# Even and odd queries laid out by DMA, and the gelu's last product moved from VectorE to GpSimd

## The chip, the core and the metric

The kernel runs on one core of a Trainium2 chip. Five instruction streams run side by side on the core and meet only at semaphores: PE (TensorE, matrix products and transposes), DVE (VectorE), ACT (ScalarE), POOL (GpSimd) and SP (SyncE), which here issues all DMAs. The metric is the time of one execution on the device in microseconds.

## What is computed

128 samples, each a 128 x 256 float32 matrix `x` with a context of the same shape. Cross attention with 16 heads of 16 columns comes first, then a block that is applied to three quarters of the rows of each sample:

```python
x = x + xattn(layernorm(x), ctx_1024, Wq, bq, Wkv, bkv, Wo, bo)
x = x + ffn(layernorm(x), w_router, w_block)

# xattn
q = (input @ Wq + bq);  k, v = split(encoded_features @ Wkv + bkv)
attn = softmax(q @ k.T / math.sqrt(16), axis=2)      # per head
return (attn @ v) @ Wo + bo
# ffn
scores = einsum('bld,d->bl', x, w_router)
top_idx = top_k(scores, 96)
out = x.at[top_idx].set(gelu(selected @ w_block))    # gelu: tanh form
```

## The kernel before, in words

One loop counter `s` runs from -10 to 144 on every engine, and in each step every engine does one piece of work for several samples at different stages: `scores(s)` on PE, `exps(s, j)` on ACT, `projection(s - 2)`, `block_product(s - 4)`, `final(s - 16)` on DVE and so on. Each engine's program is written out in this fixed order; nothing is scheduled at run time. A step therefore means one sample through the loop.

For the scores, four row groups of 32 partitions of PE work at once. Each group holds two heads (an even and an odd one) of one column half. To get both heads' scores from one product, `q_eo` holds the queries twice: once with the rows of odd heads zero and once with the rows of even heads zero. `q_raw` (queries plus bias) is written by DVE (`queries`, L597) for a pair of samples, and POOL multiplies it twice by `head_mask` (L764), which is 0 or 1/4, the scale of the softmax. `scores` (L292) reads `q_eo` three steps later.

The maxima of the scores (L539) are on DVE, in four parts j = 3, 2, 1, 0 per sample, and ACT's exponentials (L462) wait for each. ACT also copies attention, x1 and the transposed inputs out of PSUM.

The gelu of the block's result is spread over POOL and ACT: square (L797), factor (L804) and cubic product (L811) on POOL in step b + 5, tanh on ACT (L495) in step b + 7, and `gelu_product` (L639) on DVE in step b + 8: (tanh + 1) x z in one instruction with two inputs in SBUF. `final` (L680) on DVE in step b + 16 puts it together with the rows that are not processed (`unprocessed`, L828, on POOL).

Once for each group of 8 samples DVE finds the rows to drop (`router`): ten small steps over several values of `s`; rounds 6 to 9, the last with `keep_row` (L666), fall into one value of `s`. PE then turns `keep_row` into columns (L427).

SP loads x and context for two samples at a time and stores two samples at a time, each in the order of its own queue; each of its DMAs can wait for a semaphore, and what stands behind waits too.

Of the kernel before, what the change touches and what calls it, by code (L numbers as in the profile page):

```python
# [6 lines left out]
def cross_attention_routed_ffn(  # L7
# [20 lines left out]
    B, T, E = x.shape  # L28
# [19 lines left out]
    with ctx:  # L48
# [13 lines left out]
        q_eo = sb("q_eo", [P, 2, C, 2, 2, T])  # L62
# [19 lines left out]
        head_mask = sb("head_mask", [P, 2])  # L82
# [62 lines left out]
        parity_ready = sem("parity_ready")  # L145
        head_mask_ready = sem("head_mask_ready")
# [12 lines left out]
        q_eo_ready = sem("q_eo_ready")  # L159
# [21 lines left out]
        gelu_ready = sem("gelu_ready")  # L181
# [17 lines left out]
        def _(sp):  # L199
# [22 lines left out]

            load_x(0)
# [17 lines left out]
            for s in range(-7, LAST + 1):  # L241
                if s > -6:
                    load_c(s + 8)
                store(s - 17)
                load_x(s + 13)
# [4 lines left out]
        def _(pe):  # L250
# [22 lines left out]
            def scores(b):  # L273
# [4 lines left out]
                if h == 0:  # L278
                    pe.wait_ge(q_eo_ready, upto(b + 1))
                    pe.wait_ge(k_ready, upto(b + 1))  # L280
# [8 lines left out]
                for c in range(C):  # L289
                    for j in range(J):  # L290
                        rows = slice(32 * j, 32 * j + 32)
                        mm = nc.tensor.matmul(ps_s[:, bank(b, j), c, :, :], k_sb[rows, r2, c, h * T:(h + 1) * T],  # L292
                                              q_eo[rows, r2, c, h, :, :], start=True, stop=True)
# [151 lines left out]
        def _(act):  # L445
            def weights_high(s):
                for n, first in WEIGHTS:
                    if s == first:
                        act.wait_ge(w_in[n], 16)
                        nc.scalar.copy(w_hi[n][:, :, :], raw_w[n]).then_inc(w_hi_ready[n], 1)  # L450
# [58 lines left out]
        def _(dve):  # L509
            nc.vector.memset(v_pad[:, :, :, :, :], 0.0).then_inc(v_pad_zero, 1)  # L510

            dve.wait_ge(const_ready, 1)
            nc.vector.tensor_reduce(head_mask[:, :], ident[:, :].rearrange("p (g q d) -> p q g d", q=2, d=D), AX.XY,
                                    ALU.add).then_inc(parity_ready, 1)
            dve.wait_ge(parity_ready, 1)
            nc.vector.tensor_scalar(head_mask[:, :], head_mask[:, :], SCALE, None, ALU.mult).then_inc(head_mask_ready, 1)

            def weights_low(s):
                for n, first in WEIGHTS:
                    if s == first:  # L520
                        dve.wait_ge(w_hi_ready[n], 1)
                        nc.vector.tensor_tensor(w_lo[n][:, :, :], raw_w[n], w_hi[n][:, :, :].bitcast(f32),
                                                ALU.subtract).then_inc(w_lo_ready[n], 1)
# [65 lines left out]
            def queries(b):  # L589

                if b % 2 == 0 and has(b):
                    dve.wait_ge(q_mm, upto(b + 1))
                    if has(b - 4):
                        dve.wait_ge(q_eo_ready, upto(b - 3))
                    if b == 0:
                        dve.wait_ge(b_in, 64)
                    nc.vector.tensor_tensor(q_raw[:, (b // 2) % 2, :, :, :].rearrange("p c b t -> p c (b t)"),  # L597
# [36 lines left out]

            def gelu_product(b):

                if has(b):
                    dve.wait_ge(tanh_ready, upto(b))
# [228 lines left out]
```

## Time and profile before

| what | us |
|---|---|
| median of 3 runs | 970.96 |
| lowest and highest run | 969.74, 970.99 |
| the profiled execution | 971.5 |
| its span, first to last instruction | 969.6 |
| mean granted TensorE clock, share of full speed | 0.986 |

The profile gives each instruction's start and length and the event that ended the idle time before it. "Busy" is the time in which an engine has an instruction in progress; ACT's and PE's instructions overlap, so their lengths add up to more than their busy time. Timeline rows read: start, length, engine, line, operation, what is written from what. Rows from SPq are DMA issues on SP's queue. Busy time by itself does not say what bounds the loop, since the engines wait for each other within a step.

### The profile page before, as it was taken

To read this page: it belongs to the slowest core of one execution; us is meant where nothing else is said; L and a number is where in the kernel's file an instruction comes from. 1 tells how busy PE (TensorE), PEld (TensorE's weight loads), DVE (VectorE), ACT (ScalarE), POOL (GpSimd) and SP (SyncE) were. 2 spreads that over 40 slices of the span, in tenths; PEclk is the share of its full clock that TensorE was granted. 3 is DMA by queue.
4 is the path that set the end of the run, shared out by engine and by line. 5 is a ranking of instruction groups with operands and counts; after the bars stand their busy time and mean duration, and the time that the engine had idled before them with its cause. 6 is when DMAs were issued, how large, how long until landed. Compare 5 with 4: busy or idle time off the path is not lost. (4 is left out here: it accounts for less than half of the span.)

```text
span 969.6 us, 32620 instructions
## 1 busy us (share of the span) xinstructions
PE 901.8 (93%) x10276; PEld 756.4 (78%) x10276; DVE 916.4 (95%) x2696; ACT 898.4 (93%) x4612; POOL 827.0 (85%) x1386
## 2 busy tenths in 40 slices
PE   3799999999999999999999999999999999999971
PEld 3688888878788888888888887888878788788750
DVE  4689999999999999999999999999999999999975
ACT  2699999999999999999999999999999999999970
POOL 5567889999898898989989899998989999998757
PEclk9899999999999999999999999999999999999995
DMA  7010111122122122112212212211211221210002
GB/s 213 5 45 24 45 46 52 50 67 68 34 67 67 36 67 67 49 54 67 67 35 67 67 34 67 67 47 55 67 48 55 67 67 35 67 46 23 13 24 87
DMA packets 54857, 53.99 MB, mean 56 GB/s; under 512 B 4000, under 2 KB 54688, under 8 KB 54688
## 3 DMA queue, kind: packets, MB, share of 16 engines
q1 hardware_dynamic: 54688, 51.92, 17.0%
q8 instruction: 84, 1.38, 0.6%
q14 instruction: 85, 0.70, 0.2%
HBM read 35.13 MB, written 16.78 MB: 54 GB/s over the span
## 5 line engine op out<-in xcount | busy, mean ns | idle before, releaser
L462 ACT ACTIVATE e_sb<-ps_s,neg_max 128x128 f32<-128x128 f32 x2048 | 717.5, 413 | 14.9 <-DVE neg_max L539 14.6
L462 ACT ACTIVATION_READ_ACCUMULATOR e_sb<-ps_s,neg_max 128x1 f32 x2048 | 516.3, 253 | 0.0
L539 DVE TENSOR_REDUCE neg_max<-ps_s 128x4 f32<-128x512 f32 x512 | 328.0, 660 | 21.0 <-PE ps_s L292 19.3
L292 PE MATMUL ps_s<-q_eo,k_sb 32*128 32x256 f32 x2048 | 147.6, 401 | 8.8 <-ACT e_sb L462 5.3
L764 POOL TENSOR_TENSOR q_eo<-q_raw,head_mask 128x512 f32<-128x512 f32 x128 | 141.5, 1124 | 2.6 <-PE ps_t L313 1.6
L265 PE MATMUL ps_a<-w_o_sb,o_sb 128*128 128x256 f32 x512 | 137.6, 391 | 5.4 <-DVE v_sb L621 2.7
L776 POOL TENSOR_TENSOR v_pad<-v_sb,recip 128x256 f32<-128x256 f32 x128 | 79.4, 620 | 71.7 <-DVE recip L577 71.3
L341 PE MATMUL ps_a<-e_sb,v_pad 128*32 128x128 f32 x4096 | 138.4, 276 | 0.7 <-DVE x_sb L547 0.6
L265 PE MATMUL ps_t<-w_z_sb,xt_sb 128*128 128x258 f32 x512 | 134.0, 384 | 3.6 <-DVE z_sb L632 3.6
L292 PEld LDWEIGHTS ps_s<-q_eo,k_sb 32*128 32x128 f32 x2048 | 96.3, 185 | 38.0 <-issue 36.5
L341 PEld LDWEIGHTS ps_a<-e_sb,v_pad 128*32 128x32 f32 x4096 | 104.1, 109 | 22.4 <-issue 21.3
L753 POOL TENSOR_TENSOR x_sb<-x_sb,bo_sb 128x256 f32<-128x256 f32 x128 | 106.6, 833 | 9.5
L265 PEld LDWEIGHTS ps_t<-w_z_sb,xt_sb 128*128 128x128 f32 x512 | 96.0, 191 | 20.0 <-issue 4.9
L265 PEld LDWEIGHTS ps_a<-w_o_sb,o_sb 128*128 128x128 f32 x512 | 86.9, 189 | 21.1 <-issue 11.8
L811 POOL TENSOR_TENSOR g_sb<-g_sb,z_sb 128x256 f32<-128x256 f32 x128 | 99.4, 776 | 0.8
L473 ACT CAST t_hi<-ps_t 128x512 fp32r<-128x512 f32 x128 | 76.0, 594 | 25.1 <-PE ps_t L313 23.9
L584 DVE TENSOR_TENSOR t_lo<-ps_t,t_hi 128x512 fp32r<-128x512 f32 x128 | 86.6, 676 | 1.8 <-ACT t_hi L473 1.8
L258 PE MATMUL ps_a<-w_v_hi,t_hi 128*128 128x256 f32 x256 | 83.6, 327 | 2.7 <-ACT o_sb L481 2.5
L639 DVE SCALAR_TENSOR_TENSOR z_sb<-g_sb,z_sb 128x256 f32<-128x256 f32 x128 | 84.0, 657 | 0.0
L744 POOL TENSOR_SCALAR xhat<-x_sb,neg_m,rstd 128x256 f32<-128x256 f32 x128 | 81.9, 640 | 0.1
L797 POOL TENSOR_TENSOR g_sb<-z_sb 128x256 f32<-128x256 f32 x128 | 79.0, 617 | 3.1 <-DVE z_sb L632 3.0
L680 DVE SCALAR_TENSOR_TENSOR z_sb<-z_sb,half_keep,x_sb 128x256 f32<-128x256 f32 x128 | 72.1, 564 | 7.0 <-POOL x_sb L828 7.0
(80 smaller groups left out, 2252.2 us busy)
## 6 DMA issues: line engine op xcount, KB each, us to landing
x_sb<-in_x SPq DMA_DIRECT2D x64, 256.0 KB, 3.0
c_sb<-in_ctx SPq DMA_DIRECT2D x64, 256.0 KB, 3.1
out<-z_sb SPq DMA_DIRECT2D x64, 256.0 KB, 2.2
z_sb<-in_L_xattn_Wkv SPq DMA_DIRECT2D x2, 256.0 KB, 5.7
z_sb<-in_L_xattn_Wq SPq DMA_DIRECT2D x1, 256.0 KB, 3.0
w_o_sb<-in_L_xattn_Wo SPq DMA_DIRECT2D x1, 256.0 KB, 7.5
w_z_sb<-in_L_ffn_w_block SPq DMA_DIRECT2D x1, 256.0 KB, 5.6
bv_sb<-in_L_xattn_bkv SPq DMA_DIRECT2D x1, 128.0 KB, 3.5
```

What stands on the lines that cost most here:

```text
L258: last = nc.tensor.matmul(dst, lhs(a, c), rhs(b, c), start=(c == 0 and n == 0), stop=(c == C - 1 and n == len(terms) - 1))
L265: last = nc.tensor.matmul(dst, lhs(c), rhs(c), start=(c == 0), stop=(c == C - 1))
L292: mm = nc.tensor.matmul(ps_s[:, bank(b, j), c, :, :], k_sb[rows, r2, c, h * T:(h + 1) * T], q_eo[rows, r2, c, h, :, :], start=True, stop=True)
L341: mm = nc.tensor.matmul(ps_attn[32 * j:32 * j + 32, c * T:(c + 1) * T], v_pad[:, b % 2, c * J + j, par:par + 2, :].rearrange("p a d -> p ( ...
L462: last = nc.scalar.activation(e_sb[:, b % 4, j, c, par, :], ps_s[:, bank(b, j), c, par, :], ACT.Exp, bias=neg_max[:, b % 4, h:h + 1], accu ...
L539: nc.vector.tensor_reduce(neg_max[:, b % 4, :].rearrange("p (c j q) -> p j c q", c=C, j=J)[:, j, :, :], ps_s[:, bank(b, j), :, :, :], AX.X ...
L584: nc.vector.tensor_tensor(t_lo[part].rearrange("p k c t -> p (k c) t"), ps_t[:, :].rearrange("p (n t) -> p n t", t=T), t_hi[part].rearrang ...
L639: nc.vector.scalar_tensor_tensor(z_sb[:, b % R, 0:E], g_sb[:, b % 4, :], 1.0, z_sb[:, b % R, 0:E], ALU.add, ALU.mult).then_inc(gelu_ready, 1)
L744: nc.gpsimd.tensor_scalar(xhat[:, b % 4, :], x_sb[:, r, :], neg_m1[:, r:r + 1], rstd1[:, r:r + 1], ALU.add, ALU.mult).then_inc(xhat_ready, 1)
L753: nc.gpsimd.tensor_tensor(x_sb[:, b % R, :], x_sb[:, b % R, :], bo_sb[:, :], ALU.add).then_inc(xb_ready, 1)
L764: last = nc.gpsimd.tensor_tensor(q_eo[:, n, :, :, par, :], q_raw[:, n, :, :, :], head_mask[:, par:par + 1].rearrange("p (a b c) -> p a b c ...
L811: nc.gpsimd.tensor_tensor(g_sb[:, b % 4, :], g_sb[:, b % 4, :], z_sb[:, b % R, 0:E], ALU.mult).then_inc(cubic_ready, 1)
```

## The change

The layout of `q_eo` becomes parity first, so that one head parity's rows are contiguous in a partition (2 KB). It is zeroed once by DVE. For each pair of samples, SP then copies the 16 partitions of each parity of each row group from `q_raw` into it: 8 DMAs of 16 partitions x 512 elements. The scale 1/4 moves into the weights (`w_hi`, `w_lo`) and the bias of the queries; `head_mask` goes. `queries` waits for the DMAs of the pair before it in the same buffer, and `scores` for all eight. `gelu_product` leaves DVE; POOL gets `gelu_sum` (tanh + 1, in place) and `gelu_product`, both in step b + 7.

```diff
-        q_eo = sb("q_eo", [P, 2, C, 2, 2, T])
+        q_eo = sb("q_eo", [P, 2, 2, C, 2, T])
...
+            def queries_even_odd(b):
+
+                if b % 2 == 0 and has(b):
+                    n = (b // 2) % 2
+                    if b == 0:
+                        sp.wait_ge(q_eo_zero, 1)
+                    sp.wait_ge(q_raw_ready, upto(b + 1))
+                    if has(b - 4):
+                        sp.wait_ge(s_mm[J - 1], upto(b - 3))
+                    for par in range(2):
+                        for j in range(J):
+                            rows = slice(32 * j + D * par, 32 * j + D * par + D)
+                            sp.dma_start(q_eo[rows, n, par, :, :, :], q_raw[rows, n, :, :, :]).then_inc(q_eo_in[n], 16)
...
             for s in range(-7, LAST + 1):
+                queries_even_odd(s + 3)
                 if s > -6:
                     load_c(s + 8)
                 store(s - 17)
...
-                    pe.wait_ge(q_eo_ready, upto(b + 1))
+                    pe.wait_ge(q_eo_in[r2], (b // 4 + 1) * 128)
...
-                                              q_eo[rows, r2, c, h, :, :], start=True, stop=True)
+                                              q_eo[rows, r2, :, c, h, :], start=True, stop=True)
...
-                        nc.scalar.copy(w_hi[n][:, :, :], raw_w[n]).then_inc(w_hi_ready[n], 1)
+                        nc.scalar.activation(w_hi[n][:, :, :], raw_w[n], ACT.Copy,
+                                             scale=SCALE if n == "q" else 1.0).then_inc(w_hi_ready[n], 1)
...
-            dve.wait_ge(const_ready, 1)
-            nc.vector.tensor_reduce(head_mask[:, :], ident[:, :].rearrange("p (g q d) -> p q g d", q=2, d=D), AX.XY,
-                                    ALU.add).then_inc(parity_ready, 1)
-            dve.wait_ge(parity_ready, 1)
-            nc.vector.tensor_scalar(head_mask[:, :], head_mask[:, :], SCALE, None, ALU.mult).then_inc(head_mask_ready, 1)
+            nc.vector.memset(q_eo[:, :, :, :, :, :], 0.0).then_inc(q_eo_zero, 1)
...
                     if has(b - 4):
-                        dve.wait_ge(q_eo_ready, upto(b - 3))
+                        dve.wait_ge(q_eo_in[(b // 2) % 2], b // 4 * 128)
                     if b == 0:
                         dve.wait_ge(b_in, 64)
+                        nc.vector.tensor_scalar(bq_sb[:, :], bq_sb[:, :], SCALE, None, ALU.mult).then_inc(bq_scaled, 1)
+                        dve.wait_ge(bq_scaled, 1)
...
-            def gelu_product(b):
-
-                if has(b):
-                    dve.wait_ge(tanh_ready, upto(b))
-                    nc.vector.scalar_tensor_tensor(z_sb[:, b % R, 0:E], g_sb[:, b % 4, :], 1.0, z_sb[:, b % R, 0:E],
-                                                   ALU.add, ALU.mult).then_inc(gelu_ready, 1)
...
                 stats1(s + 10)
-                gelu_product(s - 8)
                 aggregate2(s - 3)
...
-                    for par in range(2):
-                        last = nc.gpsimd.tensor_tensor(q_eo[:, n, :, :, par, :], q_raw[:, n, :, :, :],
-                                                       head_mask[:, par:par + 1].rearrange("p (a b c) -> p a b c", a=1, b=1).to_broadcast([P, C, 2, T]),
-                                                       ALU.mult)
-                    last.then_inc(q_eo_ready, 2)
...
+            def gelu_sum(b):
+
+                if has(b):
+                    pool.wait_ge(tanh_ready, upto(b))
+                    nc.gpsimd.tensor_scalar(g_sb[:, b % 4, :], g_sb[:, b % 4, :], 1.0, 1.0,
+                                            ALU.add, ALU.mult).then_inc(gelu_sum_ready, 1)
+
+            def gelu_product(b):
+
+                if has(b):
+                    pool.wait_ge(gelu_sum_ready, upto(b))
+                    nc.gpsimd.tensor_tensor(z_sb[:, b % R, 0:E], g_sb[:, b % 4, :], z_sb[:, b % R, 0:E],
+                                            ALU.mult).then_inc(gelu_ready, 1)
...
                 gelu_factor(s - 5)
+                gelu_sum(s - 7)
                 input_and_bias(s + 4)
                 gelu_cubic(s - 5)
-                queries_even_odd(s + 3)
+                gelu_product(s - 7)
```

POOL in the middle of the program, before, from one `v_pad` to the next, in a step of odd number (names are written tile, then what it is computed from; `x2` is two in a row):

```order
L776 TENSOR_TENSOR v_pad<-v_sb,recip 128x8x2x16
L828 TENSOR_SCALAR x_sb<-x_sb,alpha,beta 128x256
L804 TENSOR_SCALAR g_sb<-g_sb 128x256
L753 TENSOR_TENSOR x_sb<-x_sb,bo_sb 128x256
L811 TENSOR_TENSOR g_sb<-g_sb,z_sb 128x256
L764 TENSOR_TENSOR q_eo<-q_raw,head_mask 128x4x128 x2
L744 TENSOR_SCALAR xhat<-x_sb,neg_m,rstd 128x256
```

The same place of POOL after the change (each step has these rows):

```order
L768 TENSOR_TENSOR v_pad<-v_sb,recip 128x8x2x16
L834 TENSOR_SCALAR x_sb<-x_sb,alpha,beta 128x256
L796 TENSOR_SCALAR g_sb<-g_sb 128x256
L810 TENSOR_SCALAR g_sb<-g_sb 128x256
L758 TENSOR_TENSOR x_sb<-x_sb,bo_sb 128x256
L803 TENSOR_TENSOR g_sb<-g_sb,z_sb 128x256
L817 TENSOR_TENSOR z_sb<-g_sb,z_sb 128x256
L749 TENSOR_SCALAR xhat<-x_sb,neg_m,rstd 128x256
```

The two `q_eo` rows of every second step are gone; L810 and L817, the sum and the product of the gelu, stand in every step.

SP in the middle, before, for two pairs of samples:

```order
L213 DMA c_sb<-in_ctx 128x2x256
L220 DMA out<-z_sb 128x2x256
L205 DMA x_sb<-in_x 128x2x256
L213 DMA c_sb<-in_ctx 128x2x256
L220 DMA out<-z_sb 128x2x256
L205 DMA x_sb<-in_x 128x2x256
```

SP at the same place after:

```order
L212 DMA c_sb<-in_ctx 128x2x256
L234 DMA q_eo<-q_raw 16x512 x8
L219 DMA out<-z_sb 128x2x256
L204 DMA x_sb<-in_x 128x2x256
L212 DMA c_sb<-in_ctx 128x2x256
L234 DMA q_eo<-q_raw 16x512 x8
L219 DMA out<-z_sb 128x2x256
L204 DMA x_sb<-in_x 128x2x256
```

Eight small DMAs stand ahead of each pair's store and load of x.

POOL near the end, after the change, from the last square on:

```order
L789 TENSOR_TENSOR g_sb<-z_sb 128x256
L834 TENSOR_SCALAR x_sb<-x_sb,alpha,beta 128x256
L796 TENSOR_SCALAR g_sb<-g_sb 128x256
L810 TENSOR_SCALAR g_sb<-g_sb 128x256
L803 TENSOR_TENSOR g_sb<-g_sb,z_sb 128x256
L817 TENSOR_TENSOR z_sb<-g_sb,z_sb 128x256
L834 TENSOR_SCALAR x_sb<-x_sb,alpha,beta 128x256
L810 TENSOR_SCALAR g_sb<-g_sb 128x256
L817 TENSOR_TENSOR z_sb<-g_sb,z_sb 128x256
L834 TENSOR_SCALAR x_sb<-x_sb,alpha,beta 128x256
L810 TENSOR_SCALAR g_sb<-g_sb 128x256
L817 TENSOR_TENSOR z_sb<-g_sb,z_sb 128x256
```

Before, three of the `x_sb` rows (L828) followed each other here without a gelu instruction between them.

## Rows read from the trace of the kernel before

**Rows 1.** part 1 of the page, busy us and share of each engine
```profile
PE 901.8 (93%) x10276; PEld 756.4 (78%) x10276; DVE 916.4 (95%) x2696; ACT 898.4 (93%) x4612; POOL 827.0 (85%) x1386
```

**Rows 2.** windows: length, busy us of PE, PEld, DVE, ACT, POOL; clock, DMA
```profile
63.37:132.37 69.00, 68.39 (x805) 58.45 (x801) 62.58 (x181) 68.74 (x361) 55.51 (x95) 1.00 0.13 40
139.44:888.74 749.30, 731.90 (x8428) 615.06 (x8428) 744.71 (x2196) 734.16 (x3783) 677.54 (x1127) 1.00 0.18 56
```

**Rows 3.** timeline of PE: start us, us, the scores of six samples
```profile
63.37 1.15 PE L292 MATMUL ps_s<-q_eo,k_sb 32*128 32x256 f32 x16
...
132.37 1.15 PE L292 MATMUL ps_s<-q_eo,k_sb 32*128 32x256 f32 x16
...
139.44 1.15 PE L292 MATMUL ps_s<-q_eo,k_sb 32*128 32x256 f32 x16 [0.15 <-issue]
...
538.66 1.15 PE L292 MATMUL ps_s<-q_eo,k_sb 32*128 32x256 f32 x16
...
546.95 1.15 PE L292 MATMUL ps_s<-q_eo,k_sb 32*128 32x256 f32 x16
...
888.74 1.15 PE L292 MATMUL ps_s<-q_eo,k_sb 32*128 32x256 f32 x16
```

**Rows 4.** timeline of DVE in the long step
```profile
539.25 0.74 DVE L666 TENSOR_SCALAR keep_row<-cand 8x128 f32<-8x128 f32 x1
...
540.25 1.11 DVE L639 SCALAR_TENSOR_TENSOR z_sb<-g_sb,z_sb 128x256 f32<-128x256 f32 x1
...
541.50 1.24 DVE L539 TENSOR_REDUCE neg_max<-ps_s 128x4 f32<-128x512 f32 x2
```

**Rows 5.** ACT in the long step; then waits: us in total, times, longest
```profile
542.18 0.37 ACT L462 ACTIVATE e_sb<-ps_s,neg_max 128x128 f32<-128x128 f32 x1 [1.16 <-DVE neg_max L539]
...
ACT e_sb L462 <- DVE neg_max L539: 14.6, 15, 1.2
```

**Rows 6.** timeline of DVE, an early step; idle before it in brackets
```profile
92.17 1.29 DVE L539 TENSOR_REDUCE neg_max<-ps_s 128x4 f32<-128x512 f32 x2 [0.68 <-PE ps_s L292]
```

**Rows 7.** groups of 300:700 us: busy us, mean ns of one
```profile
L764 POOL TENSOR_TENSOR q_eo<-q_raw,head_mask 128x512 f32<-128x512 f32 x56 | 62.1, 1127 | 0.0
L811 POOL TENSOR_TENSOR g_sb<-g_sb,z_sb 128x256 f32<-128x256 f32 x56 | 44.0, 787 | 0.0
L639 DVE SCALAR_TENSOR_TENSOR z_sb<-g_sb,z_sb 128x256 f32<-128x256 f32 x56 | 38.2, 683 | 0.0
L804 POOL TENSOR_SCALAR g_sb<-g_sb 128x256 f32<-128x256 f32 x56 | 22.7, 405 | 4.7
```

**Rows 8.** waits of POOL, 139.44:888.74: us in total, times, longest
```profile
POOL v_pad L776 <- DVE recip L577: 42.3, 65, 1.5
```

**Rows 9.** SP's queue in a step; then DMA issues, us to landing
```profile
525.26 0.50 SPq L213 DMA_DIRECT2D c_sb<-in_ctx  x1
...
x_sb<-in_x SPq DMA_DIRECT2D x64, 256.0 KB, 3.0
out<-z_sb SPq DMA_DIRECT2D x64, 256.0 KB, 2.2
```

**Rows 10.** timelines of DVE, PE and DVE at the start
```profile
21.64 0.69 DVE L597 TENSOR_TENSOR q_raw<-ps_q,bq_sb 128x512 f32<-128x512 f32 x1 [1.31 <-PE ps_q L258]
...
27.93 1.15 PE L292 MATMUL ps_s<-q_eo,k_sb 32*128 32x256 f32 x16
...
28.71 0.42 DVE L565 BATCH_NORM_STATS2 st<-x_sb 128x6 f32<-128x256 f32 x1
```

**Rows 11.** timelines of POOL and DVE in the drain
```profile
946.16 0.19 POOL L787 TENSOR_TENSOR ve<-mv,eps_sb 128x2 f32<-128x2 f32 x1 [1.58 <-DVE mv L559]
...
954.77 3.15 POOL L828 TENSOR_SCALAR x_sb<-x_sb,alpha,beta 128x256 f32<-128x256 f32 x3
...
958.92 0.21 DVE L666 TENSOR_SCALAR keep_row<-cand 8x128 f32<-8x128 f32 x1
...
960.31 6.04 POOL L828 TENSOR_SCALAR x_sb<-x_sb,alpha,beta 128x256 f32<-128x256 f32 x8
```

More of the change, by code:

```diff
@@ L81, in cross_attention_routed_ffn @@
         minus_mean = sb("minus_mean", [P, P])
-        head_mask = sb("head_mask", [P, 2])
         eps_sb = sb("eps_sb", [P, 2])
@@ L144, in cross_attention_routed_ffn @@
         v_pad_zero = sem("v_pad_zero")
-        parity_ready = sem("parity_ready")
-        head_mask_ready = sem("head_mask_ready")
+        bq_scaled = sem("bq_scaled")
         w_hi_ready = {n: sem(f"w_{n}_hi_ready") for n in "qkv"}
@@ L158, in cross_attention_routed_ffn @@
         q_raw_ready = sem("q_raw_ready")
-        q_eo_ready = sem("q_eo_ready")
+        q_eo_zero = sem("q_eo_zero")
+        q_eo_in = [sem(f"q_eo_in{i}") for i in range(2)]
         k_mm = sem("k_mm")
@@ L180, in cross_attention_routed_ffn @@
         tanh_ready = sem("tanh_ready")
-        gelu_ready = sem("gelu_ready")
+        gelu_ready, gelu_sum_ready = sem("gelu_ready"), sem("gelu_sum_ready")
         score_mm = sem("score_mm")
@@ L521, in weights_low @@
                         dve.wait_ge(w_hi_ready[n], 1)
-                        nc.vector.tensor_tensor(w_lo[n][:, :, :], raw_w[n], w_hi[n][:, :, :].bitcast(f32),
-                                                ALU.subtract).then_inc(w_lo_ready[n], 1)
+                        nc.vector.scalar_tensor_tensor(w_lo[n][:, :, :], raw_w[n], SCALE if n == "q" else 1.0,
+                                                       w_hi[n][:, :, :].bitcast(f32), ALU.mult,
+                                                       ALU.subtract).then_inc(w_lo_ready[n], 1)
                 if s == 0:
@@ L723, in _ @@
                                     pattern=[[-1, P]], channel_multiplier=1).then_inc(const_ready, 1)
-            pool.wait_ge(head_mask_ready, 1)
             pool.wait_ge(v_pad_zero, 1)
@@ L754, in input_and_bias @@
                                             ALU.add).then_inc(xb_ready, 1)
-            def queries_even_odd(b):
-                if b % 2 == 0 and has(b):
-                    pool.wait_ge(q_raw_ready, upto(b + 1))
-                    if has(b - 4):
-                        pool.wait_ge(s_mm[J - 1], upto(b - 3))
-                    n = (b // 2) % 2
-                    for par in range(2):
-                        last = nc.gpsimd.tensor_tensor(q_eo[:, n, :, :, par, :], q_raw[:, n, :, :, :],
-                                                       head_mask[:, par:par + 1].rearrange("p (a b c) -> p a b c", a=1, b=1).to_broadcast([P, C, 2, T]),
-                                                       ALU.mult)
-                    last.then_inc(q_eo_ready, 2)
             def values_over_sums(b):
```

## The prediction

> **What bounds the kernel now.** I read part 1 of the page first. PE, ACT and DVE are each busy for 93 to 95% of the span and POOL for 85% [rows 1], so no share names the bound; the stage has to be read. The middle of the program is 105 steps, from the scores that start at 139.44 to those at 888.74 [rows 3]: 749.3 us, 7.136 a step. In it DVE is busy for 744.7 us, 99.4%, ACT for 734.2, POOL for 677.5 [rows 2]. An earlier stretch shows the same loop before the router and the final step begin: ten steps from 63.37 to 132.37 take 69.00 us, 6.90 a step. There ACT is busy for 68.74 of 69.00 us, and DVE sits idle before its first maximum of a step (0.68 us in the row) [rows 2, 3, 6]. So ACT, with its 16 exponentials and four copies a sample, sets a floor of 6.90, and in the middle DVE adds to it.
>
> Where it adds: once per group of 8 samples the four router instructions (last two rounds and keep_row) fall into one step, and that step takes 8.29 us instead of about 6.9 (538.66 to 546.95) [rows 3]. DVE comes to its maxima only at 541.50, behind keep_row (0.74) and the gelu product (1.11) [rows 4], and ACT waits 1.16 us for neg_max; all such waits sum to 14.6 us, 15 times, and 12 of them have this length [rows 5]. The other 93 steps take (749.3 - 12 x 8.29) / 93 = 6.987.
>
> **Taken from DVE.** One gelu product a step, 56 in the stretch of 400 us at 683 ns [rows 7]. DVE's need falls from 744.7 / 105 = 7.09 us a step to 6.41, under the floor of 6.90. In the router step the product that goes is 1.11 us long [rows 4], almost all of the 1.16 that ACT waits, and DVE no longer enters that step late. So the step time should fall to between 6.90 (ACT's floor) and 6.987 plus nothing (ordinary steps keep their present length, the 12 long ones become ordinary). The ordinary steps' excess of 0.09 has one cause that I can see, a DVE with no idle time, so part of it should go as well; I take the middle, 6.945. That gives 105 x 6.945 = 729.2, a gain of 20.1. The ends are 24.8 (6.90) and, with 6.987 and a remainder of 0.3 in each of 12 groups, 749.3 - 733.6 - 3.6 = 12.
>
> **POOL: out and in.** Out go two q_eo products for every two samples, 1127 ns each, so 1.13 a step. In come gelu_sum, which has the form of the gelu factor (405 ns), and gelu_product, which has the form of the cubic product (787 ns) [rows 7], with some 0.08 for one more hand-over: 1.27. POOL's present need is its busy time and its gaps without the waits for recip: (749.3 - 42.3) / 105 = 6.73 [rows 2, 8]. After: 6.73 - 1.13 + 1.27 = 6.87. This is 0.03 under ACT's floor, so the bound moves from one engine to nearly two. The load also becomes even, where q_eo stood in every second step only. The wait for v_pad has a cushion, since attention is PE's last work of a step.
>
> POOL's cubic product and DVE's gelu product show each other's presence: the product's mean is 683 ns and reaches 1.11 us beside q_eo [rows 4, 7]. The Trainium skill (SBUF — State Buffer, Who interferes with whom) says that a DVE instruction with two SBUF inputs and a GpSimd instruction that reads SBUF exclude each other for their whole length. By that rule, the trace agrees, removing the product from DVE also shortens POOL's own rows; the sum stays, the chance of the POOL rival falls.
>
> **Queries by DMA.** Eight DMAs of 32 KB for each pair replace the POOL work; the mask and the scale are prepared once in weights and bias, at no steady cost. SP issues them ahead of the store and of load_x. An issue occupies SP for about 0.5 us [rows 9], so 8 take 4 us of the 13.9 us that a pair lasts, and SP has nothing else but three issues. q_raw of sample s+3 is written in step s and read in step s+3: at least two whole steps, 13.8 us, lie between, and 4 + 3.0 us for a landing [rows 9] fit. No row shows an SBUF to SBUF DMA; the nearest are the 256 KB ones with 2.2 and 3.0 us. The bound below is nothing, above is 13.8 - 7 = 6.8 us of room. Behind these issues wait the store and the loads; these have three steps until their use, so 4 us are hidden. If that cover went, each pair would pay what is over. PE reads q_eo in two pieces of 128 columns, now 2 KB apart, instead of 256 in a row. No row has such a read; I take zero, and PE, under its full load, could hide little above that.
>
> **Start.** q_raw(0) starts at 21.64 and is done at 22.3; two small steps for the scaled bias add 0.2. Eight issues end at 26.5, and the landing (2.2 to 3.0) makes q_eo(0) ready at 28.2 to 29.5, where scores(0) start at 27.93 today. The load of x(10) queues behind them and lands at 26.6 + 3.0 = 29.6, where DVE reads it at 28.71 [rows 9, 10]. The first maxima stand behind it. From here to the first exponentials nothing is idle in their favour, so this costs 0.3 to 2 us; I take 1.0. DVE's memset of q_eo is over about when x(0) lands.
>
> **Drain.** After the last scores POOL's own chain sets the end: it waits for DVE at 946.16 (1.58 us), and then works without a wait to the last of three u products at 957.92; keep_row follows at 958.92 and then eight more u products [rows 11]. Here each added pair of gelu instructions (0.405 + 0.08 + about 0.70) lies on the path, since z, the candidates and the last router rounds wait for DVE's final, and that for u. Five such pairs lie between 946.16 and the last of the three u (those of steps 130 to 134): 5 x 1.19 = 5.95. Against it stands that the three u take 3.15 us today, because DVE's chain beside them is slow, where three of eight later ones would take 3 x 0.755 = 2.27, and that four gelu products leave DVE. I take 4.5, with 2 and 5 as ends.
>
> **Sum.** -20.1 + 1.0 + 4.5 = -14.6. The profiled execution has a span of 969.6 and 971.5 us with what lies around it; the median of the runs is 970.96, 0.5 lower. So the span becomes 955.0, the profiled time 956.9, and the median 956.4.
>
> **Rivals.** (1) POOL becomes the bound. For it: 6.87 stands next to 6.90, and its rows stretch when others run beside them (the cubic product's mean of 787 ns). At 7.0 a step: 105 x 7.0 = 735.0, gain 14.3, median 970.96 - 14.3 + 5.5 = 962.2. Against: the wait for recip today sums to 42.3 us and the work added is 0.14 a step, 15 us in 105 steps. The Trainium skill (GPSIMD Engine Reference, 4.1 Engine selection) speaks against the move: elementwise work belongs on VectorE, since GpSimd takes about twice as long for two inputs. An estimate by that page, 2 x 683 ns for the product, makes POOL's need 7.45, and the time then about 1009 us; the row of the same form says 787.
> (2) Slower: POOL's need passes 7.10. There the middle takes 105 x 7.10 = 745.5, a gain of 3.8 that start and drain (5.5) more than eat; at 7.25 the middle takes 761.3 and the time is 970.96 + 12 + 5.5 = 988. The point is reached where POOL's five two-input instructions a step (square, v_pad, bias, cubic, product) stretch by 0.05 each beyond their present means. Nothing in the rows suggests it, but the slack is thin.
> (3) SP's queue becomes the bound: 11 issues in 13.9 us allow 1.26 us each. At 1.4 us, 64 pairs x 1.5 us = +96 us. The row says 0.5.
> (4) Only the long steps shrink and the ordinary ones keep 6.987 with a remainder: gain 12 to 15.6, median 961 to 964.
> That the change doesn't do what it says is out: the order of POOL and SP shows it.
>
> **Chances.** Forecast 0.55; (1) 0.17; (4) 0.14; (2) 0.07; (3) 0.02; a gain eaten until within 0.2% 0.05. The predicted time is 956.4. The range must hold the forecast's own ends (24.8 - 2.3 = 22.5, so 948.5; 12 - 7 = 5, so 966) and rivals (1) and (4): 949 to 966. About 2 us, 0.2%, is what a measurement can tell from no change. Faster 0.87, same 0.05, slower 0.08.
>
> **What would show it.** In the middle, the step of 8.29 should be gone and ACT's wait for neg_max with it; the step near 6.94; ACT busy above 99%; DVE idle again before its first maximum; POOL busy at about 95%, with q_eo rows gone and its wait for recip short but there. SP's eight issues of 0.5 us should end well ahead of the scores. The first scores should start near 28.9, and the span from the last neg_max to the end should be 4 to 5 us longer, with POOL in the chain. Wrong would be: waits of PE for v_pad or for a DMA, POOL without waits at over 6.95 a step, or the product at over 0.9 us.

## The result and the profile after

| | before | after |
|---|---|---|
| median of 4 runs, us | 970.35 | 957.89 |
| lowest and highest run | 969.64, 970.99 | 957.61, 958.20 |
| ratio after / before, 95% interval | | 0.9875 [0.9861, 0.9890] |
| span of the profiled execution | 969.6 | 956.0 |
| granted TensorE clock | 0.986 | 0.985 |

The change is faster by 1.25%, 12.5 us in the medians; the two profiled executions lie 13.6 us apart in their spans, because the profiled one of the kernel before was about 1 us above its median. The profile shows where. First part 1 of the page of the kernel after (busy us and share of each engine, answering [rows 1]), then the window over the same 105 steps of the middle (length; busy us of PE, PEld, DVE, ACT, POOL; clock, DMA share, GB/s; answering the second line of [rows 2]):

```profile
PE 892.5 (93%) x10276; PEld 757.0 (79%) x10276; DVE 849.6 (89%) x2568; ACT 894.6 (94%) x4612; POOL 814.4 (85%) x1514
```
```profile
140.22:871.17 730.95, 724.02 (x8427) 616.81 (x8427) 687.53 (x2091) 729.83 (x3783) 666.37 (x1231) 1.00 0.27 77
```

The 105 steps take 730.95 us, 6.961 each, where they took 749.30. DVE fell from 99.4% to 94.1% of the stretch. The scores of a router group, from the timeline of PE (start, length, engine, line, operation):

```profile
592.81 1.15 PE L306 MATMUL ps_s<-q_eo,k_sb 32*128 32x256 f32 x16
599.74 1.15 PE L306 MATMUL ps_s<-q_eo,k_sb 32*128 32x256 f32 x16
606.52 1.15 PE L306 MATMUL ps_s<-q_eo,k_sb 32*128 32x256 f32 x16
613.61 1.15 PE L306 MATMUL ps_s<-q_eo,k_sb 32*128 32x256 f32 x16 [0.16 <-issue]
```

The pattern of a group is 7.12, 6.93, 6.78, 7.09, 6.88, 6.98, 6.78, 7.09; the step of 8.29 [rows 3] is gone. ACT waits for neg_max 1.0 us in the whole program, where one such wait was 1.16 [rows 5]. DVE now waits for the scores before its first maximum, also in the middle, and POOL still waits a little for recip (waits of the 105 steps, 140.22:871.17: us in total, times, longest):

```profile
DVE neg_max L551 <- PE ps_s L306: 38.1, 69, 0.9
POOL v_pad L768 <- DVE recip L589: 37.1, 91, 1.4
```

The groups of the stretch 300:700 us (busy us, mean ns of one, idle before), as in [rows 7]: the new product is L817, the new sum L810, the cubic product L803, the bias addition L758, the step's one DVE instruction that still reads two tiles of SBUF is `final`, L687.

```profile
L758 POOL TENSOR_TENSOR x_sb<-x_sb,bo_sb 128x256 f32<-128x256 f32 x58 | 57.7, 994 | 0.0
L803 POOL TENSOR_TENSOR g_sb<-g_sb,z_sb 128x256 f32<-128x256 f32 x58 | 40.7, 702 | 0.0
L817 POOL TENSOR_TENSOR z_sb<-g_sb,z_sb 128x256 f32<-128x256 f32 x58 | 39.4, 680 | 0.0
L687 DVE SCALAR_TENSOR_TENSOR z_sb<-z_sb,half_keep,x_sb 128x256 f32<-128x256 f32 x57 | 30.1, 528 | 0.0
L810 POOL TENSOR_SCALAR g_sb<-g_sb 128x256 f32<-128x256 f32 x57 | 23.2, 407 | 4.6
```

The queries' DMAs on SP's queue in the middle, and the page's row on their issues (count, KB each, median us from issue to landing), answering [rows 9]:

```profile
541.83 5.55 SPq L234 DMA_DIRECT2D q_eo<-q_raw  x8
547.42 0.58 SPq L219 DMA_DIRECT2D out<-z_sb  x1
```
```profile
q_eo<-q_raw SPq DMA_DIRECT2D x512, 32.0 KB, 2.0
```

Eight issues take 5.55 us here, 0.69 each. After the store and the two loads SP then issues nothing for 6.5 us until the next eight, and no wait of PE for them stands in the middle.

The start (answering [rows 10]), from the timelines of SP and of PE:

```profile
21.99 5.01 SPq L234 DMA_DIRECT2D q_eo<-q_raw  x8
```
```profile
28.42 1.15 PE L306 MATMUL ps_s<-q_eo,k_sb 32*128 32x256 f32 x16 [1.29 <-DMA q_eo<-q_raw]
```

The drain (answering [rows 11]), from the timeline of POOL:

```profile
929.32 0.20 POOL L779 TENSOR_TENSOR ve<-mv,eps_sb 128x2 f32<-128x2 f32 x1 [0.39 <-DVE mv L571]
...
940.53 0.56 POOL L834 TENSOR_SCALAR x_sb<-x_sb,alpha,beta 128x256 f32<-128x256 f32 x1
941.05 0.40 POOL L810 TENSOR_SCALAR g_sb<-g_sb 128x256 f32<-128x256 f32 x1
941.54 0.77 POOL L817 TENSOR_TENSOR z_sb<-g_sb,z_sb 128x256 f32<-128x256 f32 x1
...
943.99 0.55 POOL L834 TENSOR_SCALAR x_sb<-x_sb,alpha,beta 128x256 f32<-128x256 f32 x1
```

The last scores start at 911.41 (before 929.13), so 44.6 us lie behind them, where 40.5 did. In the drain POOL waits 0.39 us instead of 1.58 and then works through to the last of the three u rows (943.99 + 0.55), with a sum and a product between each two of them.

The account of the span: middle -18.35; start +0.78 (scores number 16 start at 140.22 instead of 139.44); the six steps between the middle and the last scores -0.15 (40.24 instead of 40.39); drain +4.1. Together -13.6, which is 956.0 - 969.6. Of the 18.35, 12 x (8.29 - 7.12) = 14.0 come from the twelve long steps, which are now steps of 7.12, and 4.3 from the other 93, which went from 6.987 to (730.95 - 12 x 7.12) / 93 = 6.941.

### The profile page after: what moved, and what is told of

It is laid out like the page before. It is cut to its first block, busy times and chain, and to the rows that moved or that the text cites. A ratio compares the mean times of both kernels' runs of the same rounds, so it can differ in the third digit from the quotient of the medians.

```text
span 956.0 us, 33133 instructions
## 1 busy us (share of the span) xinstructions
PE 892.5 (93%) x10276; PEld 757.0 (79%) x10276; DVE 849.6 (89%) x2568; ACT 894.6 (94%) x4612; POOL 814.4 (85%) x1514
## 4 chain that ended last, share of the span: by engine, by line
PE 88%; ACT 5%; issue 2%; POOL 2%; DVE 1%; SPq 1%; DMA 1%; POOLq 0%; ACTq 0%; DVEq 0%
PE ps_q L272 18%; PE ps_s L306 14%; PE ps_a L355 13%; PE ps_a L279 12%; PE ps_t L279 11%; PE ps_a L272 9%; PE ps_t L327 8%; ACT e_sb L477 4%; PE ps_q L342 3%; DMA x_sb<-in_x 1%; POOL x_sb L834 1%; SPq L234 0%; POOL z_sb L817 0%; DVE neg_max L551 0%; PE ps_t L441 0%
## 5 line engine op out<-in xcount | busy, mean ns | idle before, releaser
L477 ACT ACTIVATE e_sb<-ps_s,neg_max 128x128 f32<-128x128 f32 x2048 | 724.9, 459 | 1.2 <-DVE neg_max L551 1.0
L477 ACT ACTIVATION_READ_ACCUMULATOR e_sb<-ps_s,neg_max 128x1 f32 x2048 | 588.3, 299 | 0.0
L551 DVE TENSOR_REDUCE neg_max<-ps_s 128x4 f32<-128x512 f32 x512 | 332.0, 669 | 64.4 <-PE ps_s L306 62.2
L758 POOL TENSOR_TENSOR x_sb<-x_sb,bo_sb 128x256 f32<-128x256 f32 x128 | 121.3, 947 | 0.2
L488 ACT CAST t_hi<-ps_t 128x512 fp32r<-128x512 f32 x128 | 80.9, 632 | 25.0 <-PE ps_t L327 23.8
L803 POOL TENSOR_TENSOR g_sb<-g_sb,z_sb 128x256 f32<-128x256 f32 x128 | 90.7, 709 | 0.0
L817 POOL TENSOR_TENSOR z_sb<-g_sb,z_sb 128x256 f32<-128x256 f32 x128 | 87.6, 684 | 0.2
L510 ACT ACTIVATE g_sb<-g_sb 128x256 f32<-128x256 f32 x128 | 74.1, 579 | 8.2 <-POOL g_sb L803 8.2
L687 DVE SCALAR_TENSOR_TENSOR z_sb<-z_sb,half_keep,x_sb 128x256 f32<-128x256 f32 x128 | 67.7, 529 | 11.5 <-POOL x_sb L834 11.5
L834 POOL TENSOR_SCALAR x_sb<-x_sb,alpha,beta 128x256 f32<-128x256 f32 x128 | 73.0, 571 | 1.7
```

Of the source, the lines that this page charges most:

```text
L477: last = nc.scalar.activation(e_sb[:, b % 4, j, c, par, :], ps_s[:, bank(b, j), c, par, :], ACT.Exp, bias=neg_max[:, b % 4, h:h + 1], accu ...
L488: nc.scalar.copy(t_hi[:, n, :, :, h * T:(h + 1) * T].rearrange("p k c t -> p (k c) t"), ps_t[:, :].rearrange("p (n t) -> p n t", t=T)).the ...
L551: nc.vector.tensor_reduce(neg_max[:, b % 4, :].rearrange("p (c j q) -> p j c q", c=C, j=J)[:, j, :, :], ps_s[:, bank(b, j), :, :, :], AX.X ...
L758: nc.gpsimd.tensor_tensor(x_sb[:, b % R, :], x_sb[:, b % R, :], bo_sb[:, :], ALU.add).then_inc(xb_ready, 1)
L803: nc.gpsimd.tensor_tensor(g_sb[:, b % 4, :], g_sb[:, b % 4, :], z_sb[:, b % R, 0:E], ALU.mult).then_inc(cubic_ready, 1)
L817: nc.gpsimd.tensor_tensor(z_sb[:, b % R, 0:E], g_sb[:, b % 4, :], z_sb[:, b % R, 0:E], ALU.mult).then_inc(gelu_ready, 1)
```

## The experiments

Two things were open after this. The change has two halves, and DVE's need falls by both (the product itself; the q_eo products that stretch DVE's rows). And the prediction says that ACT is the floor and POOL next to it. Each kernel's scores were read in the same way as above: "middle" is the 105 steps from scores number 16 on, "drain" what lies from the last scores to the end of the span. Ratios are to the kernel before, with the 95% interval. One-run times have no interval. Four chips were used: a first for the DMA half alone, the move alone and the kernel before without the product; a second for the full change again, the full change with more POOL, the one with the last 8 products on DVE and the DMA half with the load of x(10) first; a third for the DMA half alone again, the two kernels with POOL's two extra instructions and the one without tanh; a fourth for both repairs. The full change reads 957.89 and 955.90 in its two timings, so 2 us between rows of different chips say nothing by themselves.

| kernel | median us (runs) | ratio | middle | drain |
|---|---|---|---|---|
| before | 970.3 to 971.3 | 1 | 749.3 | 40.5 |
| full change | 957.89 (4) | 0.9875 [0.9861, 0.9890] | 730.95 | 44.6 |
| full change, again | 955.90 (4) | 0.9849 [0.9835, 0.9862] | 729.5 | 43.6 |
| DMA half alone | 955.23 (4) | 0.9841 [0.9825, 0.9858] | 729.7 | 41.6 |
| DMA half alone, again | 954.98 (5) | 0.9848 [0.9835, 0.9861] | 730.8 | 40.4 |
| move alone | 1000.99 (1) | | 777.4 | 43.8 |
| before without the product | 952.51 (4) | 0.9810 [0.9796, 0.9825] | 731.0 | 40.5 |
| DMA half, POOL keeps reading | 971.76 (1) | | 749.35 | 40.4 |
| DMA half, POOL only writes | 959.47 (1) | | 737.2 | 40.4 |
| full change, more POOL | 959.05 (1) | | 729.4 | 47.0 |
| full change without tanh | 950.68 (1) | | 725.95 | 43.6 |
| full change, last 8 products on DVE | 952.56 (4) | 0.9816 [0.9803, 0.9830] | 729.2 | 40.5 |
| DMA half, load of x(10) first | 951.83 (5) | 0.9809 [0.9796, 0.9822] | 729.4 | 40.4 |
| both repairs on the full change | 953.81 (5) | 0.9832 [0.9819, 0.9846] | 731.0 | 40.5 |

### The DMA half alone

```diff
             for s in range(FIRST, LAST):
                 stats1(s + 10)
+                gelu_product(s - 8)        # one instruction on DVE, as before
...
-                gelu_sum(s - 7)
...
-                gelu_product(s - 7)
```

> The queries are laid out by DMA as in the changed kernel; the gelu product stays on DVE in one instruction, in step b + 8. Theory (DVE was the bound, and part of its length was waiting beside POOL's q_eo products): the product shortens from 683 ns to about 0.45 us, keep_row from 0.74 to about 0.2, the step of 8.29 us loses most of its excess, the ordinary steps stay near 6.99. Middle 105 x 7.0 = 735, gain 14, start +0.8, no longer drain: median about 957 to 960, and DVE busy still 97% or more. Rival A (DVE's rows have their lengths in any case, the DMA part only makes room on POOL): the product stays at 0.65 us or more, the long step stays at 8.2, median 970 to 972. Rival B (POOL's q_eo was the bound): ACT is busy in over 98.5% of the middle and DVE gets idle time, median below 955.

Measured: 955.23 us, and 954.98 when repeated; below the 957 to 960 of the theory, since the ordinary steps shrank too. The window of the 105 steps (columns as above) of the repeated run:

```profile
140.68:871.46 730.78, 725.73 (x8427) 617.23 (x8428) 721.56 (x2195) 730.03 (x3783) 554.50 (x1021) 1.00 0.27 77
```

DVE still does the product and is busy 98.7% of the stretch, yet the steps are as short as with the full change. The product on DVE lasts 414 ns in place of the 683 of [rows 7]. So the DMA half carries the whole gain of the middle. For DVE's length of a step, taking POOL's q_eo products away did what taking the product away was meant to do.

> The same kernel as e1_dma_alone, timed again with more rounds since its four runs lay between 952.9 and 955.5. Theory (its middle equals that of the full change and its drain is 4 us shorter; the moved load at the start is worth little, as scores(2) start at 43.0 against 43.3 in the traces): 951.5 to 953 us, 3 to 4 us below the full change's 955.9. Rival (the first median was its level, and the moved load is worth 3 us): 954.5 to 955.5.

The 954.98 is the rival's value, not the theory's. Against its kernel before, the DMA half alone is at 0.9841 and 0.9848, the full change at 0.9875 and 0.9849: no gain of the product's move can be seen on top of the DMA half, in the time or in the middle.

### The product's move alone, and the product left out

```diff
-                gelu_product(s - 8)        # DVE
...
+                gelu_sum(s - 7)            # POOL, beside the q_eo products
+                gelu_product(s - 7)
```

> The queries stay on POOL; only the gelu's sum and product move to POOL. Theory (POOL had 6.73 us of work in a step of 7.14): POOL's need becomes 6.73 + 0.41 + 0.68 + 0.08 = 7.9 us a step, POOL has no wait for recip left, PE and ACT wait for it: middle 105 x 7.9 = 830, median 1045 to 1065. Rival (POOL has more room than its rows say, since rows overlap the waits): median 957 to 975.

Measured: 1000.99 us in one run, against 971.32 for the kernel before on that chip, between the two ranges that were written down; steps of 7.40 in the mean. The waits of the middle (us in total, times, longest) show the rival that the full change escaped, POOL as the bound:

```profile
DVE z_sb L673 <- POOL x_sb L834: 68.7, 52, 1.6
...
PE ps_a L341 <- POOL v_pad L768: 39.2, 51, 1.1
```

POOL has no wait in it; its rows, with what waiting they hold, fill the 7.40 us. The move by itself is thus 3% slower, and it is borne only where the DMA half goes with it; even there it brings nothing in the middle (729.5 to 731.0 against 729.7 to 730.8) and lengthens the drain. The step of 7.9 that I had written was too long; some of POOL's own rows were shorter than in [rows 7]: the cubic product 682 ns, not 787, q_eo 1039, not 1127.

```diff
-                gelu_product(s - 8)        # DVE; no other engine does it
```

> The kernel before with the gelu's last product left out altogether (that part of the computation is missing), q_eo on POOL as before. Theory (DVE was the bound, POOL's load of 6.73 is below the floor of 6.90): the step of 8.29 goes, steps of 6.93 to 6.96, middle 728 to 731, gain 18 to 21 with nothing lost at the start and 0 to 2 us won in the drain: median 949 to 953. Rival (the gain of the changed kernel came from POOL's relief of q_eo, not from DVE): little change, 964 to 971.

This kernel leaves out the gelu's last product, so its result isn't the reference's.

Measured: 952.51 us, as the theory had it, the middle 731.0. keep_row still lasts 0.74 there, so the product's 1.11 us was enough to take the long step away. With q_eo still on POOL, taking the product from DVE also gives the step of 6.96. Either half of the relief is enough for the middle. They are not two gains that add up.

### Is it POOL's reading that stretches DVE?

Both kernels are the DMA half alone, with two more POOL instructions for each pair of samples, where the q_eo products stood; nobody reads what they write. One pair reads `q_raw` as the q_eo products did, the other only writes. In both kernels DVE's `queries` waits for the earlier pair of them (not in the cuts below); the profile shows no wait of DVE for it in the middle of the first. The layout by DMA stays in both, so neither it nor the hand-over through POOL can be what differs.

```diff
+                    for par in range(2):
+                        last = nc.gpsimd.tensor_tensor(junk[..., par, ...], q_raw[:, n, :, :, :], eps_sb[:, par:par + 1]..., ALU.mult)
```
```diff
+                    for par in range(2):
+                        last = nc.gpsimd.memset(junk[:, n, 1024 * par:1024 * par + 1024], 0.0)
```

> As e1_dma_alone, but POOL still multiplies q_raw twice a pair at its old place, into a tile that nobody reads. Theory (two products of POOL that read SBUF hold back the gelu product and keep_row on DVE): the product is back at 0.65 to 0.7 us, the step of 8.2 to 8.3 us is back once in 8, middle 745 to 750, median 968 to 973. Rival (it was the hand-over through POOL, or the layout, that cost): as e1_dma_alone, 951 to 956.

> As e13_pool_keeps_reads, but POOL's two idle instructions only write (memset of 1024 columns each, about 1 us each) and read nothing from SBUF. Theory (DVE's instruction with two SBUF inputs and POOL's reads exclude each other, writes alone don't): the product stays near 0.42 us, no long step, steps 6.96, median 951 to 956. Rival (any work of POOL beside DVE stretches it, or POOL's time counts as such): as e13_pool_keeps_reads, 965 to 973.

Measured, one run each: 971.76 us with the reads, in the theory's range; 959.47 with writes only, between the theory's range and the rival's. With the reads the gain is gone to the last tenth. The middle takes 749.35 us (before 749.30), the group has its step of 8.28 again. The timeline of PE, then of DVE and of POOL in that step:

```profile
539.34 1.15 PE L307 MATMUL ps_s<-q_eo,k_sb 32*128 32x256 f32 x16
547.62 1.15 PE L307 MATMUL ps_s<-q_eo,k_sb 32*128 32x256 f32 x16
```
```profile
539.92 0.74 DVE L682 TENSOR_SCALAR keep_row<-cand 8x128 f32<-8x128 f32 x1
...
540.92 1.11 DVE L655 SCALAR_TENSOR_TENSOR z_sb<-g_sb,z_sb 128x256 f32<-128x256 f32 x1
```
```profile
539.54 2.22 POOL L779 TENSOR_TENSOR junk<-q_raw,eps_sb 128x512 f32<-128x512 f32 x2
```

These are the 0.74 and the 1.11 of [rows 4]. In the same place of the kernel without POOL's two products the timeline of DVE reads:

```profile
530.98 0.21 DVE L680 TENSOR_SCALAR keep_row<-cand 8x128 f32<-8x128 f32 x1
...
531.46 0.40 DVE L653 SCALAR_TENSOR_TENSOR z_sb<-g_sb,z_sb 128x256 f32<-128x256 f32 x1
```

The ends line up. POOL's first product ends at 539.54 + 1.11 = 540.65, and keep_row, issued at 539.92, ends at 540.66. POOL's second ends at 541.76, and DVE's product ends 0.27 behind it. So each of the two DVE instructions comes to its end only behind the POOL instruction that it met. In the long step that was 0.53 + 0.71 = 1.24 us, for a wait of ACT of 1.16. (keep_row beside other rows of POOL takes 0.27 in most groups of the kernel without the two products, and 0.43 in the full change.)

With writes only the middle takes 737.2. The product on DVE stays short (449 ns in the mean; of the 57 between 300 and 700 us, 25 lie beside a memset alone and last 0.40), but keep_row is held up, in some groups by both memsets:

```profile
532.53 1.84 POOL L779 MEMSET junk<- 128x1024 f32 x2
```
```profile
532.92 1.52 DVE L682 TENSOR_SCALAR keep_row<-cand 8x128 f32<-8x128 f32 x1
```

Here keep_row ends at 534.44, 0.07 behind the memsets, and a product issued behind it (533.39, 1.05 us) ends with it: a row can also hold the wait of the row ahead of it. Six of the 14 steps of the middle in this place of the group take 7.77 us, the others 7.12, where keep_row mostly takes 0.62; another step of each group takes 7.20 in place of 7.02, and why is not read here. So the theory holds for the product, and fails for keep_row. That the middle is 12 us shorter than with the reads fits a product that is no longer stretched; the memsets are also shorter than the products (0.95 against 1.13 us), and the runs don't separate the two.

The Trainium skill (SBUF — State Buffer, Who interferes with whom) has both cases: two SBUF inputs on DVE collide with a GpSimd instruction that reads SBUF and not with one that only writes, while a DVE `tensor_scalar` in a two-port mode collides with any, for the whole instruction. The rows agree for the product, 683 ns beside reads against 449. For keep_row, a `tensor_scalar`, they fit as well, 0.74 and 1.52 against 0.21 us; which mode it ran in, no row shows.

### How near is POOL to being the bound?

```diff
                     pool.wait_ge(gelu_sum_ready, ...)
+                    nc.gpsimd.tensor_scalar(g_sb[:, b % 4, :], g_sb[:, b % 4, :], 1.0, 0.0, ALU.mult, ALU.add)...
```

> The full change with one more POOL instruction of 0.41 us a step (the sum is copied onto itself). Theory (POOL's need is about 6.6 us, of the step's 6.96, the wait for recip of 0.34 us a step is its whole room): need 7.05 to 7.15, POOL's wait for recip gone, steps of about 7.05 to 7.15: median 968 to 980, drain 2 us longer among it. Rival (POOL had more room than the wait shows): steps stay at 6.96, median 959 to 961.

Measured: 959.05 us, the rival's value. The middle stays at 729.4 us, 6.95 a step (729.5 for the full change on the same chip), although 0.40 us of work were added to each step and POOL's wait for recip is 0 in the stretch 300:700. The bias addition, which stood at 994 ns in the full change (1001 on this chip), is:

```profile
L758 POOL TENSOR_TENSOR x_sb<-x_sb,bo_sb 128x256 f32<-128x256 f32 x58 | 45.5, 784 | 0.0
```

So POOL's rows hold waiting inside them, which work can take the place of. Per step, the wait for recip gave 0.33 us and this row 0.22, while the sum's row (L810) grew from 0.40 to 0.53. What the bias addition waited for can be read in the full change, from the timelines of DVE and POOL:

```profile
612.33 0.48 DVE L687 SCALAR_TENSOR_TENSOR z_sb<-z_sb,half_keep,x_sb 128x256 f32<-128x256 f32 x1
```
```profile
612.44 0.95 POOL L758 TENSOR_TENSOR x_sb<-x_sb,bo_sb 128x256 f32<-128x256 f32 x1
```

It ends 0.58 us behind `final`, DVE's other instruction with two inputs in SBUF. Between 300 and 700 us 43 of its rows start while `final` is in progress, and each ends 0.58 to 0.60 behind it. Here POOL is the one that is held up. The price of the added instruction stands in the drain alone, 47.0 us against 43.6 (on the same chip 959.05 against 955.90).

### Is ACT the floor?

```diff
-                gelu_tanh(s - 7)
...
-                    pool.wait_ge(tanh_ready, upto(b))
+                    pool.wait_ge(cubic_ready, upto(b))
```

> The full change without the tanh on ACT (left out; the sum takes the cubic product instead). Question: what bounds the steps of 6.96 that all variants reach. Theory PE (the chain of the full change's trace is 88% PE): steps stay at 6.94 to 6.96, ACT shows idle time of 0.3 us a step, median 953 to 957. Rival ACT (16 exponentials and four copies fill it): 0.32 us a step less on ACT, steps fall to PE's 6.80 or below, median 935 to 942.

This kernel leaves out the tanh, so what it computes isn't the gelu.

Measured: 950.68 us in one run, below the theory's 953 to 957 and far above the rival's; the window of the 105 steps:

```profile
138.99:864.94 725.95, 722.52 (x8428) 615.69 (x8428) 684.99 (x2091) 706.87 (x3678) 665.07 (x1231) 1.00 0.27 77
```

The step falls by 0.048 only, to 6.914, though a tanh of 0.59 us (mean of its rows in the full change) left ACT. PE is now busy for 99.5% and ACT for 97.4%, and ACT now waits for PE, where the middle of the full change shows no wait of ACT:

```profile
ACT t_hi L488 <- PE ps_t L327: 17.8, 79, 0.4
```

The pattern of a group becomes 7.12, 6.93, 6.78, 6.93, 6.88, 6.93, 6.78, 6.93: the steps of 7.09 and 6.98 shrink to 6.93 and the others keep their length. So ACT adds 0.05 to 0.16 in three steps of eight and doesn't bound the other five. PE is what is left for those: it waits for another engine once, 0.3 us, while DVE and ACT wait for it. No run took work from PE, so this is read from the trace and not tested. ACT's busy share of 99.8% in the full change did not say that: its accumulator reads have a mean of 305 ns there, 255 here, and 248 in the kernel before.

### The drain and the start

```diff
+        LATE = B - 8
...
-                if has(b):                 # gelu_sum, gelu_product on POOL
+                if 0 <= b < LATE:
...
                 router(s - 15, 9)
+                gelu_product(s - 8)        # DVE, for b >= LATE, one instruction
```

> The changed kernel, but the gelu's sum and product of the last 8 samples (120 to 127) are one instruction on DVE again, at the end of its step b + 8. Theory (the added POOL instructions lie on the chain of the drain): the time from the last scores to the end falls from 44.6 us to 40 to 41.5, the median from 957.9 to about 954 to 955. Rival (the drain's 4 us come from something else, the router's chain or the stores): median stays at 957 to 958.5.

> The full change again, beside the others on one chip, as their comparison. Theory and rival alike: 957.5 to 958.5 us, ratio to the kernel before 0.986 to 0.989; e1_dma_alone and e11_dma_alone_start are below it by 2.5 to 4 us if the drain is what the moved product costs.

Measured on the same chip: 952.56 against 955.90 us, drain 40.5 against 43.6, as the theory had the drain. The 955.90 itself is 2 us under what was expected of a repeat; its middle is 1.4 us shorter than the first time and its drain 1.0. POOL's timeline has its three u rows in one piece again:

```profile
935.03 3.15 POOL L845 TENSOR_SCALAR x_sb<-x_sb,alpha,beta 128x256 f32<-128x256 f32 x3
```

So the drain's price is that of the gelu work on POOL, and it can be had back.

```diff
             for s in range(-7, LAST + 1):
+                if s == -3:
+                    load_x(s + 13)
                 queries_even_odd(s + 3)
```

> The queries by DMA and the gelu product on DVE (as e1_dma_alone), and the load of x(10) stands ahead of the first eight q_eo DMAs on SP. Theory (DVE's first maxima waited for that load, 2.29 us in the changed kernel's trace, where the scores were only 0.5 us late): scores(1) 0.8 to 1.3 us earlier, median 0.5 to 1.3 us below e1_dma_alone's 955.2: 954 to 954.7. Rival (the late q_eo(0) sets the start): no difference, 955 to 955.5.

> The full change with both repairs together: the last eight samples' gelu product as one instruction on DVE, and the load of x(10) and x(11) ahead of the first eight q_eo DMAs. Theory A: the moved load is worth the 3 us that lay between the two kernels with the DMA alone (951.83 with it, 954.98 and 955.23 without); then the median is 952.56 - 3 = 949.5, the ratio near 0.978, and the scores with number 16 start 1 to 3 us before the 139.89 of the kernel without it. Rival B: the start differs from run to run by about a microsecond whatever this load does (scores number 16 start at 139.46 and 140.68 in two profiles of one kernel, 139.71 with the load moved); then the median stays within a microsecond of 952.5 (ratio 0.981 to 0.982), and scores number 16 start between 139.4 and 140.7. Both: 105 steps of the middle in 729 to 731 us, and 40.4 from the last scores to the end.

The DMA half with this load moved gave 951.83 us, under both expectations and 3 less than without it; but that one ran on another chip, and scores number 16 start at 139.71, and at 139.46 and 140.68 in the two profiles of the kernel without it. Put on top of the repaired drain it gave 953.81, not the 949.5 that a worth of 3 us would mean, and 0.3 above what rival B allowed; the middle is 731.0 there and scores number 16 start at 139.46. So theory A has fallen and the load's place is worth nothing that can be seen. The start has a spread of its own: scores(0) start at 27.93 before and at 26.70 with the product left out, and the two programs are the same up to there. What makes the 3 us between 951.83 and 954.98 isn't settled; the middle differs by 1.4 us of it between the profiles, and one kernel's middle read 729.7 and 730.8 in two runs. All four kernels with the DMA half on the second chip read 729.2 to 729.5, so the chip may be part of it.

## Why the prediction was right, and where it was not

The time, 957.89 for 956.4, came out inside the range, by a sum whose terms hold and whose reasons hold in part. From profile to profile the forecast was -14.6 and the measured sum -13.6: the middle gave 1.75 us less than forecast, and start, drain and the steps between together 0.8 less loss, so small misses also cancel.

**The long step.** It went, with ACT's wait, as forecast. The forecast said that the product's 1.11 us leaves the step, and the kernel without the product shows that this suffices. The runs show more: of 1.11 and 0.74 only 0.40 and 0.21 were DVE's own work, and the rest was POOL's q_eo product, which left too. I had read the two rows as showing "each other's presence" and then drew from it only a smaller chance for the POOL rival. It was what made the step long, and by it the half of the change that I costed at nothing on DVE gives the whole gain alone.

**The ordinary steps.** Forecast 6.945, measured 6.961: the gain of the middle 18.35, not 20.1, inside 12 to 24.8. The mis-sized term is the floor. ACT's 6.90 comes from before the router. In the middle the steps take 6.914 without the tanh, with two longer ones in each group (7.12, in which PE turns keep_row into columns, and 6.88, instead of 6.93 and 6.78 beside them), and ACT adds 0.05. The twelve long steps could thus fall to 7.12 and not to the "ordinary" 6.987 or less that the forecast gave them. The "excess of 0.09" that I gave to a DVE without idle time is mostly this. After the change DVE idles and the excess over 6.90 is 0.06.

**ACT above 99%.** 99.8%, as said, but no proof of a bound: without the tanh only 0.048 us a step were had.

**POOL.** Forecast need 6.87, product 787 ns, sum 405, busy 95%. Measured: (730.95 - 37.1) / 105 = 6.61, 680, 407 and 91%. Busy time less waits overstated POOL's need, in the kernel before as in the move alone (7.40 measured where 6.73 + 1.27 = 8.00), because its rows contain waiting for DVE; the bias addition shows it, 994 ns with room and 784 without, with its end tied to `final`'s. The 6.61 is for the same reason still above the true need. Rival (1) at 7.0 and rival (2) past 7.10 were further off than the 6.87 made them look: 0.40 us more did not reach the first, though it used up the wait for recip. POOL's own rows did get shorter without the product on DVE, as forecast: the cubic product has a mean of 702 ns in the full change, 787 before and 864 where the DMA half stands alone. That GpSimd takes about twice as long for two inputs (the Trainium skill, GPSIMD Engine Reference, 4.1 Engine selection) comes out here as 1.6, 680 against 414 ns. The estimate of 1009 us doubled the 683 ns, a product stretched by POOL. With its sum the work takes 1.09 us on POOL, against the 0.41 of DVE's one instruction.

**DMAs.** Landing 2.0 us against 2.2 to 3.0; an issue 0.62 to 0.69 us, not 0.5, so 5 to 5.6 us for eight, still hidden. Rival (3) did not come. PE's split read of q_eo cost nothing: the mean row of the scores in the stretch 300:700 is 399 ns before and after.

**Start.** +0.78 against +1.0, first scores at 28.42 against 28.9. The term is right in size and cannot be called shown; that it came out is luck: the same code started its first scores 1.2 us apart in two kernels, and scores number 16 start at 137.1 to 139.4 in the three kernels with q_eo on POOL and at 139.0 to 140.7 in those with the DMAs.

**Drain.** +4.1 against +4.5, in the place named: five pairs of sum and product on POOL between its last wait for DVE and the last of the three u rows. From that wait to the end of the three it took 11.76 us before and 15.22 after; POOL comes to this place 0.9 later behind the last scores (17.9 us against 17.0), and what follows the three is 0.2 shorter. The kernel with these products on DVE got all of it back.

**Rival (4)** is closer to the truth than its place as a rival suggests: the ordinary steps shrank from 6.987 to 6.941 only, 4.3 us in all, and 14.0 of the 18.35 are the long steps. Its remainder did not come, so the time stayed below its 961.

## What to carry to other kernels

When a row on DVE is longer than its kind (keep_row 0.74 against 0.21, the product 683 against 414 ns), look for the GpSimd row whose end it shares. Take that one away, and DVE has its time back without losing any of its work; here that alone gave all that the middle had to give, and the product could have stayed where it was. A busy share doesn't say what an engine needs: before an engine is called a floor or full, take a piece of its work away or add one, as ACT (0.59 less, 0.05 gained) and POOL (0.40 more, nothing lost in the loop) showed here. And price a move twice, for the loop and for the drain, where the engine that receives it may end last.

## What the runs showed of the hardware

A copy from SBUF to SBUF of 16 partitions x 2 KB lands 2.0 us after its issue, and eight in a row hold SP for 5.0 to 5.6 us. They brought the core's DMA share from 18 to 27% in the middle, at no visible cost to the loads (x lands in 2.9 us, before 3.0); stores land in 2.4 us, before 2.2. A GpSimd memset, which reads nothing, held up an 8 x 128 `tensor_scalar` of DVE from 0.21 to 0.62 us, and to 1.52 across two memsets, while the two-input product beside a memset stayed at 0.40. A GpSimd addition of 128 x 256 that starts within a two-input instruction of DVE ends 0.58 to 0.60 us behind it. On GpSimd one-input and two-input elementwise instructions of 128 x 256 take 407 and 680 ns.
